# Pacing indirect transfers by the pair loop of a routed MoE, and routing its second half earlier

## The reference, cut to what matters

```python
logits = flat @ router_w + router_bias                 # 16 experts
probs = softmax(logits); top_w, top_i = top_k(probs, 2)
norm_w = top_w / (sum(top_w) + 1e-6)
routed = combine[:, 15:16] * flat                      # the last expert is the identity
for e in range(15):
    y = silu(flat @ gate_w[e]) * (flat @ up_w[e]) @ down_w[e]
    routed += combine[:, e:e+1] * y
shared = silu(conv(x, conv_w)) * (x @ shared_up_w) @ shared_down_w
return shared + routed
```

## Time and profile before

| | |
|---|---|
| timed runs, median of 3 | 1405.84 us (1404.09 to 1406.28) |
| the profiled execution, its span | 1579.5 us |
| of it: first MoE to the end of its pairs | about 294 us |
| of it: second MoE's pairs, to the last gated product | 1307.26 to 1504.39 us |

### The profile page before, as it was taken

How to read it: one execution, slowest core, us unless ns; L and a number is a source line. 1 busy time by engine, 2 the same in 40 slices (tenths; PEclk the granted TensorE clock), 3 DMA queues, 4 the chain that set the end, 5 groups by cost and what they waited for, 6 DMA issues and landing times.

```text
span 1579.5 us, 30698 instructions
## 1 busy us (share of the span) xinstructions
PE 1351.4 (86%) x11824; PEld 1104.9 (70%) x11824; DVE 1011.0 (64%) x2391; ACT 614.6 (39%) x1034; POOL 571.9 (36%) x460
## 2 busy tenths in 40 slices
PE   6871968876999999999998999999999676496885
PEld 3461968644788888888886888888887446496753
DVE  5661536658977877777768778797787453253623
ACT  5630635422333433343344334424455262263410
POOL 0726033352342323224424443364343704304252
PEclk9975979989999999999999999999999788698998
DMA  9963559650000000000010000000002463355542
GB/s 326 372 213 122 174 175 321 206 190 23 28 2 2 1 2 1 1 2 32 8 58 1 1 15 2 15 15 14 2 28 89 167 229 131 124 181 171 156 150 90
DMA packets 113867, 151.63 MB, mean 96 GB/s; under 512 B 12224, under 2 KB 96192, under 8 KB 113728
## 3 DMA queue, kind: packets, MB, share of 16 engines
q1 hardware_dynamic: 99328, 114.02, 21.8%
q0 software_dynamic: 12288, 33.57, 6.6%
q10 hardware_dynamic: 2112, 2.10, 0.4%
HBM read 78.21 MB, written 71.43 MB: 95 GB/s over the span
## 4 chain that ended last, share of the span: by engine, by line
PE 53%; DVE 16%; another core or an unknown queue 8%; issue 2%; ACT 2%; POOL 0%; DVEq 0%; ACTq 0%
PE l_w_ps L83 8%; PE l_w_ps L85 7%; PE l_w_ps L84 7%; DVE l_probs L2221 4%; PE l_banks L2505 3%; PE l_rm_ps L2537 2%; PE l_banks L83 2%; PE l_banks L84 2%; PE l_banks L85 2%; DVE l_f_lo L2252 2%; PE l_rm_ps L2530 2%; DVE l_full L2174 1%; PE b_gu_ps L83 1%; PE b_t_ps L1284 1%
## 5 line engine op out<-in xcount | busy, mean ns | idle before, releaser
L2221 DVE TENSOR_TENSOR l_probs<-l_banks,l_past 128x512 f32<-128x512 f32 x256 | 160.1, 684 | 29.8 <-PE l_banks L2505 29.7
L1964 ACT ACTIVATE l_act_f<-l_w_ps,l_ffn_b 128x512 f32<-128x512 f32 x120 | 82.7, 690 | 169.0 <-PE l_w_ps L85 163.9
L83 PE MATMUL l_w_ps<-l_w_hi,l_f_hi 128*128 128x256 f32 x496 | 143.6, 290 | 2.6 <-DVE l_f_lo L2252 2.4
L84 PE MATMUL l_w_ps<-l_w_lo,l_f_hi 128*128 128x256 f32 x496 | 139.6, 281 | 0.0
L85 PE MATMUL l_w_ps<-l_w_hi,l_f_lo 128*128 128x256 f32 x496 | 139.5, 281 | 0.0
L2059 POOL TENSOR_TENSOR l_g_lo<-l_q,l_g_hi 128x1024 fp32r<-128x1024 f32 x16 | 39.1, 2447 | 266.9 <-ACT l_g_hi L1955 266.9
L813 POOL DMA_INDIRECT b_picked<-rows,b_pos_i x64 | 61.1, 955 | 137.4 <-DMA rows<-b_yb 88.5
L83 PE MATMUL l_w_ps<-l_b_hi,l_w_hi 128*128 128x512 f32 x240 | 102.2, 426 | 0.3 <-ACT l_f_hi L1965 0.3
L83 PEld LDWEIGHTS l_w_ps<-l_w_hi,l_f_hi 128*128 128x128 f32 x496 | 93.3, 188 | 8.8 <-issue 8.7
L2252 DVE TENSOR_TENSOR l_f_lo<-l_act_f,l_f_hi 128x512 fp32r<-128x512 f32 x128 | 85.9, 703 | 18.5 <-ACT l_f_hi L1965 18.4
L2046 POOL TENSOR_TENSOR l_q_wide<-l_q,l_pair_mask 128x1024 f32<-128x1024 f32 x32 | 60.1, 1899 | 103.7 <-DVE l_q L2189 100.0
(11 more groups left out here) (432 smaller groups left out, 4053.0 us busy)
## 6 DMA issues: line engine op xcount, KB each, us to landing
rows<-a_zeros SPq DMA_DIRECT2D x14, 1024.0 KB, 10.7
a_xb<-rows SPq DMA_DIRECT2D x46, 256.0 KB
rows<-a_yb SPq DMA_DIRECT2D x46, 256.0 KB
b_xb<-rows SPq DMA_DIRECT2D x46, 256.0 KB
rows<-b_yb SPq DMA_DIRECT2D x46, 256.0 KB
a_w_in<-in_moe_w SPq DMA_DIRECT2D x15, 384.0 KB, 10.2
low_dram<-a_w_lo SPq DMA_DIRECT2D x15, 384.0 KB
b_w_lo<-low_dram SPq DMA_DIRECT2D x15, 384.0 KB
```

The source lines that it names most:

```text
L83: tensor.matmul(out, w_hi, x_hi, start=start, stop=False)
L84: tensor.matmul(out, w_hi, x_lo, start=False, stop=False)
L1964: nc.scalar.activation(act_f[:, f, :], hidden_ps(b, f), ACT.Gelu, bias=ffn1_b[:, b.layer, f:f + 1]).then_inc(act_done, 1)
L2221: dve.tensor_tensor(probs[c % 2][:, r * w:(r + 1) * w].rearrange("p (h n) -> p h n", n=P), banks[:, r, :].rearrange("p (h n) -> p h n", n= ...
```

## The change

Three things. Each transfer of the second half's scatter first waits for the pair loop: transfer c, k = 0 for the gated product of pair 1 + 19c//16, and k = 1 for the low part of the same pair. Each transfer of the first half's picks waits likewise for pair 26 + 18c//16. And the second half's routing starts ahead of the first pair: `count(1)` goes from PE's first pair to ahead of `turn_x(0)`, the first two pieces of `rest()` go to ahead of `low_x(0)` and `low_x(1)`, and the pairs 0 and 1 run two pieces each. Both MoE stages are changed.

```diff
--- before.py
+++ after.py
@@ -793,6 +793,9 @@
             pool.memset(blank[:, :], 0.0).then_inc(zeroed, 1)
             pool.memset(ones[:, :], 1.0).then_inc(ones_done, 1)
 
+            def paced(n, k):
+                pool.wait_ge((h_done, h_lo_done)[k], n)
+
             def scatter(b):
                 pool.wait_ge(placed, b + 1)
                 if begins:
@@ -801,6 +804,8 @@
                     pool.wait_ge(xn_done, TILES_OF[0][-1] + 1)
                 for c in range(PARTS[b]):
                     for k in range(2):
+                        if b == 1:
+                            paced(2 + (PAIR0[1] - 4) * c // PARTS[1], k)
                         pool.indirect_dma_start(own_rows[b], bass.IndirectOffsetOnAxis(ap=pos_i[:, b, k, c:c + 1], axis=0),
                                                 normal(START[b] + c), None).then_inc(scattered[b][k], 16)
 
@@ -810,6 +815,8 @@
                 b = int(c >= START[1])
                 own = c - START[b]
                 for k in range(2):
+                    if b == 0:
+                        paced(COMBINE_FROM - 1 + (NPAIRS - COMBINE_FROM) * c // PARTS[0], k)
                     pool.indirect_dma_start(picked[:, c % PICKED, k, :], None, own_rows[b],
                                             bass.IndirectOffsetOnAxis(ap=pos_i[:, b, k, own:own + 1], axis=0)).then_inc(picked_in[c % PICKED], 16)
 
@@ -1139,7 +1146,9 @@
                 mark(1)
                 shared_product(2)
                 later = rest()
+            next(later)
             low_x(0)
+            next(later)
             low_x(1)
             if ends:
                 add_shared(2)
@@ -1149,7 +1158,8 @@
                 if n + 2 < NPAIRS:
                     low_x(n + 2)
                 low_h(n)
-                next(later, None)
+                for _ in range(2 if n < 2 else 1):
+                    next(later, None)
                 if n >= COMBINE_FROM and combined < PARTS[0]:
                     combine(combined)
                     combined += 1
@@ -1388,6 +1398,7 @@
                 shared_down(1)
                 turn_logits(1)
                 shared_in(2)
+            count(1)
             if begins:
                 pe.wait_ge(dve_lo_done, PIECES)
             turn_x(0)
@@ -1401,8 +1412,6 @@
                 gateup(n, at_w[n])
                 if n + 2 < NPAIRS:
                     turn_x(n + 2)
-                if n == 0:
-                    count(1)
                 if n == NPAIRS - 1:
                     turn(FRONT, True)
                 if n >= 1:
```

## The result

The changed kernel takes 1430.81 us (median of 4 runs, 1429.02 to 1432.59) beside 1406.06 for the kernel before: a ratio of 1.0175, 95% interval [1.0159, 1.0191]. It is 24.8 us slower, where 6 were forecast. Two further comparisons, on two chips, gave 1430.4 beside 1405.79 and 1436.4 beside 1406.64. The profiled execution took 1429.74 us and has a span of 1428.0, not the 1534 that I had worked out.

What follows compares the result with a forecast made beforehand. PE was taken to bound the kernel, with 53% of the chain of waits. Routing 1.5, scatter 5.0 and picks 3.6, less 3.8 regained, made +6.3 on 1405.8: 1412 us, range 1388 to 1420.

Steps and rivals of the forecast that it cites:

- the 1534: Forecast span of the changed kernel's profiled execution: 1579.5 - 55.6 + 10.1 us.
- The reading of the bursts: Pair loops under indirect-transfer bursts: stalls lie in the profiled execution, at most 7% of the unexplained time in timed runs.
- 107.4 us: Time lost in the profile at four places of the two MoE pair loops, under second scatter and first picks.
- the relief of 3.8: Gain of a timed run from spreading the bursts: 3.8 us, from a range of 0 to 3.8.
- The comparison of 186.5 with 173.7 us: Unexplained time in the profile, 186.5 us, set against the 173.7 by which the profiled execution exceeds the median.
- the losses are wholly real: Rival: timed runs have the pair-loop stalls too, so 55.6 us are gained and the time is 1360; chance 0.13.
- 25.9 in each MoE: Remaining profiled cost of spread transfers: 17.3 us for paced scatter columns and 8.6 for paced pick columns.
- The scatter term: Second scatter's later landing delays take_y(18) on ACT: 2.5 us per MoE, 5.0 in all, range 0 to 8.
- The picks term: Picks with one pair of lead land after their combines are due: 3.6 us in all, ends 0 and 11.
- The routing term: Routing moved ahead of the first pair: -0.5 us in the first MoE, +2.0 in the second, 1.5 together.
- The sum: Routing, scatter and picks costs, 10.1 us, less 3.8 regained: +6.3 us, for 1412.
- the two new waits: ACT's take_y(18) waiting after the scatter, 5.0 us, and combines waiting for picks, 3.6 us.

Runs made afterwards that it cites:

- experiment 4: Three altered kernels timed beside the kernel before on one chip, where the kernel before took 1580.2 us.
- the mended one: Changed kernel, last second-scatter column waiting for pair 15, first picks two pairs ahead of their combines: ratio 0.9486 (1498.86 us) beside 1580.2; elsewhere 1408.0 us.
- the kernel before with the stores first: Kernel before with store_y(16) and store_y(17) ahead of load_block(23) in SP's list: 1580.16 us beside 1580.2; elsewhere 1403.52 us.
- Pacing the picks alone with the stores first: Kernel before, first picks paced two pairs ahead of their combines, same stores ahead of load_block(23): 1550.45 us beside 1580.2; elsewhere 1403.82 us.

## Why the prediction was right or wrong

**The reading of the bursts: right for the runs compared, wrong as it was put.** I wrote that the bursts "stall the profiled execution and hardly the timed one". In the result's comparison nothing of 107.4 us is in either kernel, so the relief of 3.8 was 0 and the 1534 for the span was void. But the split was between chips, not between profiled and timed: on the chip of experiment 4 the 17 timed runs are as long as the profiled execution. The comparison of 186.5 with 173.7 us was sound, and it told that the profile was not of the kind of the timed runs; it did not tell why. The rival "the losses are wholly real" has its place there. By it the changed kernel would gain 55.6 - 10.1 = 45.5 us, and a version without the two late landings 55.6 - 1.5 = 54.1; the mended one gained 81.3. The relief was sized too small: from T(0) to T(45) the kernel before with the stores first takes 196.9 and 195.0 us on that chip and 141.4 and 133.8 on another, so 116.6 us lie in the two loops (107.4 forecast), and the mended version keeps 13.8 and 23.6 of them (25.9 in each MoE forecast). Pacing the picks alone with the stores first gained 29.8, where the holes under the picks were 17.6 + 12.7. What the changed kernel itself takes on that chip was not measured; the missed deadlines would have to cost over 80 us for it to come out slower.

**The scatter term, 5.0 forecast, 13.1 measured: the step that failed.** The mechanism was as described: scatter, load, store, `take_y(18)`. Three sizes were off. `store_y(16)` went at T(18) + 5.68 (forecast 5.2), its landing took 3.40 (2.7), and ACT was ready at T(18) + 3.44 (3.9), so it was 5.6 late and not 4.0. In the kernel before it was 1.1 late and not 1.5, with the store at T(18) + 1.28 (forecast 2.7), since its burst ended earlier against the pairs. The difference is 4.5 and not 2.5; of the 1.9 us by which the two stores lie further apart than forecast, 1.4 are the kernel before's. And the sum ended where the wait ended. PE had been idle for 4.6 us, and the pair behind it ran at a granted clock of 0.65 and 0.51: another 2.0 us in the first MoE and 2.5 in the second that no term held. My upper end, 8 for both MoEs, lacked it too.

**The picks term, 3.6 forecast, 8.9 measured.** The form was right (one pair of lead is less than what a pick needs), its time too short: 3.71 us instead of 2.86, which I had from a late pick. With 0.85 more the wait does not fall on every other column: between T(36) and T(45) DVE waits 12 times in the two MoEs, 12.8 us in all, 1.07 each, where 8 times 0.45 were assumed. 11 was the upper end.

**The routing term, +1.5 forecast, +0.4 measured**, within what can be told.

**The sum.** Forecast 1.5 + 5.0 + 3.6 - 3.8 = 6.3; by parts 0.4 + 13.1 + 8.9 = 22.4; whole 24.8, the rest within the spread of the runs. The sign held, the range to 1420 did not: it took the upper ends of the two new waits only in part, and the larger had a term left out.

## What to carry to other kernels

Where there are no holes, pacing transfers costs little as long as each lands before its use (nothing that can be told for either part alone here, 2 to 3 us for the mended whole) and gains nothing. A paced transfer's last moment is its consumer's time less the landing under the traffic of that stage, less all that stands in the queue between. Ask of a load that waits long what is queued behind it, and price a stall of PE with the slow clock that follows, not by its own length. When a profile's span and the timed runs differ by far more than what lies around the span, profile the kernel again on another chip before reasoning from either: a fix for holes that only some chips show has to be timed on one of those, and must not miss a deadline on the others.

## What the runs showed of the hardware

One of the five chips of the experiments took 1580 us for a kernel that takes 1406 on the others, and in each of its profiles in the same way: while POOL issues indirect transfers back to back, 1.27 us apart, work that PE has finished is taken up late by its consumers. In these timelines of PE and of ACT there, PE transposes a gated product (the group at 129.71), and the copy of it by ACT (`high_h`) begins at 149.96, with nothing in ACT's order ahead of it that the profile knows but `take_y` at 145.00, itself after 10.01 us of waiting for something "remote".

```profile
129.71 0.69 PE L1312 MATMUL a_low_ps<-ident,a_bh 128*128 128x128 f32 x2 [5.78 <-issue]
```

```profile
145.00 0.60 ACT L677 ACTIVATE a_yb<-a_acc_ps 128x512 f32<-128x512 f32 x1 [10.01 <-remote]
149.96 0.38 ACT L671 ACTIVATE a_bh_hi<-a_low_ps 128x256 fp32r<-128x256 f32 x1 [4.36 <-remote]
```

The trace also holds the times at which semaphores were raised. The transposes of 129.71 end at 130.40, and PE has gone on to other matmuls; the raise of the semaphore with which they release `high_h` is recorded at 149.88, 19.5 us later, and ACT begins 0.08 after it. In the profile of the earlier trace rows the transposes of `turn_x(8)` end at 118.91, and their raise is recorded at 131.97, 0.02 before SP's load: those are the 13 us that the prediction noticed. From 98 to 195 us, the four profiles with a span over 1496 hold 8 to 10 raises by PE each that are recorded more than 1 us after the end of the instruction, up to 26 us, and up to 4 in the mended version; of ACT and DVE they hold none so late, and the 15 other profiles hold none of any engine. So what comes late is PE's signal. It is not the transfers of the stores: `high_h` waits for none.

With two transfers per pair instead of a burst the loops of the mended version have no pair over 6.9 us, but they are 14 and 24 us longer than on another chip. Why PE's signals are late, and on this chip alone, stays open. So does what the recording has to do with it. Executions recorded in the same way on other chips have no holes. But in the four profiles only 5,086 to 5,347 of the 9,664 raises by transfers (16 for each of 604) are recorded, in the 15 others 9,606 to 9,644, so the recording itself went otherwise there. Every timed run is listed with a span and a clock of its core, so none is known to have run unrecorded, and no run shows what that chip takes without recording. The rule of the Trainium skill that the prediction cited (NOTIFIC — the notification-queue block, Overflow) is thus neither seen at work nor excluded on that chip.
